# One comparison for sixteen steps' one-hots in the loop of a graph layer, with the second buffer in dead attention memory

## The reference, cut to what matters

```python
def _gcn_conv(x, W, b, src, dst, norm, num_nodes):
    h = x @ W
    msgs = h[src] * norm[:, None]
    out = jax.ops.segment_sum(msgs, dst, num_segments=num_nodes)
    return out + b
h = jax.nn.relu(_gcn_conv(x, W1, b1, src, dst, norm, n))
out = _gcn_conv(h, W2, b2, src, dst, norm, n)
```

## Time and profile before

| | before |
|---|---|
| median of 3 runs | 719.45 us (718.57 to 721.18) |
| profiled execution | 719.86 us |
| its span | 718.0 us |
| PE busy | 568.2 us, 79% |
| DVE busy | 502.6 us, 70% |
| ACT busy | 349.0 us, 49% |
| comparisons for one-hots (L672) | 128, 154.9 us |

### The profile page before, as it was taken

The page is one execution under the profiler, slowest core; times in us unless marked ns, Lnnn a source line. Parts: engine busy times, 40 slices in busy tenths (PEclk is TensorE's granted clock), DMA queues, the critical chain, the costliest instruction groups (busy, mean ns, idle before and its releaser), DMA issues.

```text
span 718.0 us, 13436 instructions
## 1 busy us (share of the span) xinstructions
PE 568.2 (79%) x4970; PEld 502.2 (70%) x4970; DVE 502.6 (70%) x1104; ACT 349.0 (49%) x625; POOL 132.9 (19%) x133
## 2 busy tenths in 40 slices
PE   0979983597999999999999999997540799999600
PEld 0235442586999999997899999997530699999500
DVE  6792988736999999995656646677541677878534
ACT  0023863457777777771211113232260598999400
POOL 2000000000000000000000000447566055656600
PEclk9998997689999999999999999999755699999955
DMA  7999999800424554100046775382423255555199
GB/s 177 247 284 283 283 283 282 295 0 1 169 118 174 230 230 172 59 2 1 1 196 263 303 324 205 125 284 75 129 69 84 79 150 144 150 162 145 37 241 294
DMA packets 80157, 121.16 MB, mean 169 GB/s; under 512 B 8573, under 2 KB 68770, under 8 KB 78429
## 3 DMA queue, kind: packets, MB, share of 16 engines
q1 hardware_dynamic: 70621, 107.03, 49.2%
q0 software_dynamic: 9472, 13.27, 5.7%
HBM read 50.00 MB, written 72.21 MB: 170 GB/s over the span
## 4 chain that ended last, share of the span: by engine, by line
PE 53%; DVE 21%; DMA 9%; issue 5%; ACT 5%; POOL 3%; SPq 1%; DVEq 1%; ACTq 0%; POOLq 0%
PE psB L1260 21%; DVE hot L672 7%; PE psC L1163 4%; PE psA L1175 3%; DMA back<-expert_out 3%; PE psC L1260 3%; POOL expert_slots L559 3%; DMA xs<-expert_slots 3%; PE psD L1175 3%; DMA acc<-in_x_dram 2%; PE psB L1447 2%; PE psD L1322 2%; PE psA L1435 1%; ACT counts L1492 1%; PE psC L1461 1%
## 5 line engine op out<-in xcount | busy, mean ns | idle before, releaser
L1260 PE MATMUL psB<-hs,counts 125*128 125x256 f16 x1600 | 210.7, 274 | 0.0
L1260 PEld LDWEIGHTS psB<-hs,counts 125*128 125x128 f16 x1600 | 172.3, 140 | 0.6
L672 DVE TENSOR_TENSOR hot<-iota_j,places 128x2048 bf16<-128x2048 bf16 x128 | 154.9, 1223 | 21.3 <-PE psA L1175 13.5
L551 POOL IOTA row_of<- 128x25 f32 x1 | 0.2, 237 | 421.8 <-DVE acc L722 421.8
L566 POOL DMA_INDIRECT expert_out<-y,to_row x64 | 66.4, 1037 | 62.0 <-DVE y L1101 49.7
L559 POOL DMA_INDIRECT expert_slots<-rows,place x50 | 62.2, 1244 | 64.4 <-issue 48.2
L1492 ACT CAST counts<-psA 128x1000 f16<-128x1000 f32 x64 | 63.3, 988 | 16.4 <-PE psA L1175 16.3
L1492 ACT CAST counts<-psD 128x1000 f16<-128x1000 f32 x64 | 63.5, 993 | 13.1 <-PE psD L1175 13.1
L1175 PE MATMUL psA<-hot 128*128 128x125 bf16 x512 | 50.3, 223 | 12.9 <-DVE hot L672 7.1
L1175 PEld LDWEIGHTS psA<-hot 128*128 128x128 bf16 x512 | 38.8, 99 | 22.9 <-DVE hot L672 12.4
L1163 PE MATMUL psC<-wcat,xnT 128*125 128x512 f32 x100 | 52.4, 650 | 1.8 <-ACT xnT L1479 1.8
(11 more groups left out here) (283 smaller groups left out, 1018.0 us busy)
## 6 DMA issues: line engine op xcount, KB each, us to landing
expert_slots<-zeros SPq DMA_DIRECT2D x8, 3536.0 KB, 30.2
kept_counts<-counts SPq DMA_DIRECT2D x6, 4000.0 KB, 12.5
counts<-kept_counts SPq DMA_DIRECT2D x6, 4000.0 KB, 12.3
xs<-expert_slots SPq DMA_DIRECT2D x32, 272.0 KB, 3.1
back<-expert_out SPq DMA_DIRECT2D x5, 1120.0 KB
w_raw<-in_L_ffn_w_dram SPq DMA_DIRECT2D x2, 2048.0 KB, 13.8
acc<-in_x_dram SPq DMA_DIRECT2D x1, 2800.0 KB
out_dram<-acc SPq DMA_DIRECT2D x5, 560.0 KB
```

Source lines behind the costliest of these rows:

```text
L672: v.tensor_tensor(hot[:, slot].rearrange("p g w n s -> p (g w) n s"), iota_j[:, :, :].unsqueeze(1).to_broadcast([P, 2 * pairs, P, PAIR]), ...
L1260: m = pe.matmul(sum_bank(g, d), counts5[0:PT, buf, a, d, :], hs2[0:PT, a, :, :].rearrange("p q f -> p (q f)"), start=first, stop=last, ski ...
```

## The change

In the loop, and only there, one comparison makes the one-hots of two units (sixteen steps), 4096 elements on a partition. It needs two buffers of twice the size. One is the whole of `hot`; the other lies in the q columns of sixteen rows of `qkv`, read as bf16, each row 256 elements long and 1540 bytes from the next. The comparison raises `hot_ready` by 2 at its end. DVE waits once ahead of the loop for the q transposes, and before each pair until the unit three before the pair's first is built.

```diff
+        wide_hot = (hot[:, :, :, :, :, :].rearrange("p u g w n s -> p (u g w) n s"),
+                    qkv[:, 0:4 * UNIT // PAIR, 0:HID].bitcast(BF16).rearrange("p m (n s) -> p m n s", s=PAIR))
+
+        def hot_of(unit):
+
+            block = UNIT // PAIR * 2
+            if unit < UNITS + 2:
+                at = unit % 2
+                return wide_hot[0][:, block * at:block * at + block]
+            return wide_hot[unit // 2 % 2][:, block * (unit % 2):block * (unit % 2) + block]
...
+            def hot_pair(unit):
+
+                pairs = 2 * UNIT // PAIR
+                column = P * FIRST_ORDER[unit // UNITS] + UNIT * (unit % UNITS)
+                val = places[:, column // PAIR:column // PAIR + pairs].rearrange("p g w s -> p (g w) s")
+                v.tensor_tensor(wide_hot[unit // 2 % 2], iota_j[:, :, :].unsqueeze(1).to_broadcast([P, 2 * pairs, P, PAIR]),
+                                val.unsqueeze(2).to_broadcast([P, 2 * pairs, P, PAIR]), ALU.is_equal).then_inc(hot_ready, 2)
...
+            v.wait_ge(q_transposed, len(TILE_GROUPS))
             for i in range(CH - 1):
                 k = FIRST_ORDER[i]
                 for r in range(UNITS):
                     unit = UNITS * (i + 1) + 2 + r
-                    if unit < UNITS * CH:
-                        v.wait_ge(built, 2 * unit - 2)
-                        hot_unit(unit % 2, unit)
+                    if unit < UNITS * CH and r % 2 == 0:
+                        v.wait_ge(built, 2 * unit - 4)
+                        hot_pair(unit)
...
-                bank = 512 * (j % 2)
+                bank, hots = 512 * (j % 2), hot_of(g // 2)
                 for q in range(GROUP):
                     pair, s = (GROUP * (j % 2) + q) // PAIR, q % PAIR
-                    m = pe.matmul(ps[:, bank + KEYS * q:bank + KEYS * q + KEYS], hot[:, slot, pair, 0, :, s], hot[:, slot, pair, 1, 0:KEYS, s],
+                    m = pe.matmul(ps[:, bank + KEYS * q:bank + KEYS * q + KEYS], hots[:, 2 * pair, :, s], hots[:, 2 * pair + 1, 0:KEYS, s],
```

More of the change, by code:

```diff
@@ L230, in gps_layer @@
             counts5 = counts[:, :, :, :].rearrange("p r s (a d) -> p r a d s", d=W)
+        wide_hot = (hot[:, :, :, :, :, :].rearrange("p u g w n s -> p (u g w) n s"),
[6 more added lines that the diff above has]
+            return wide_hot[unit // 2 % 2][:, block * (unit % 2):block * (unit % 2) + block]
+        assert (UNITS + 2) // 2 % 2 == 1
         until_experts.close()
@@ L1164, in project, with build @@
                 m.then_inc(projected, 1)
-            def build(g, j, slot, ps):
+            def build(g, j, ps):
                 if j % 2 == 0:
@@ L1189, in _ @@
                         g = 2 * (n - FIRST) + j
-                        build(g, j, (n - FIRST) % 2, (psA, psD)[(n - FIRST) % 2])
+                        build(g, j, (psA, psD)[(n - FIRST) % 2])
             def spread_scales():
@@ L1284, in _ @@
                     g = 2 * UNITS * (k + 1) + j
-                    build(g, j, j // 2 % 2, (psA, psD)[j // 2 % 2])
+                    build(g, j, (psA, psD)[j // 2 % 2])
                     while 2 * UNITS * due < (len(SUM_LIST) - 6) * (j + 1):
```

## The result

The changed kernel takes 726.12 us (median of 6 runs, 723.74 to 727.13) against 718.25 us (6 runs, 716.57 to 721.18) for the kernel before beside it: 1.0107 times as long, 95% interval 1.0078 to 1.0135. Slower, as forecast, and 0.5 us above the forecast time. The profiled execution took 726.33 us, its span 724.4.

What follows compares the result with a forecast made beforehand. PE was taken to bound the loop, with DVE close behind. Terms of 5.6 + 0.6 - 0.2 gave 6.0 us, 725.9 on the profiled execution, taken as 725.6 us; range 721.5 to 731.0.

Steps and rivals of the forecast that it cites:

- What bounds the loop: In the loop, PE sets the pace, busy 21.56 of 22.44 us a chunk; every microsecond it loses reaches the end.
- The pair's duration: On DVE, one double-width comparison takes 2.29 us, with bounds of 2.13 and 2.45.
- A: Unit 10 of each chunk: the wide pair behind the group 0 addition makes PE start 0.80 us later, +5.6 in all.
- B: Boundary between chunks: the second addition starts earlier, so PE starts the next unit 0 earlier, -0.16 us.
- C: Local unit 2 of the next chunk: its pair ends late behind the sums, +0.16 us, cancelling B at six boundaries.
- D: The loop's first comparison: the wide pair ends later than ACT's counts, so PE starts 0.6 us later.
- Throughput: Rival: DVE's total work sets the pace, pairs save 0.56 us a chunk, kernel faster at 715.5 us; chance 0.03.
- No change: Rival: the pair takes at most 1.52 us, so unit 10 isn't late; 718.5 us; chance 0.05.
- Dear rows: Rival: comparisons into qkv rows cost far more than forecast; 729.8 us, or some 732.2 by the skill's rate; chance 0.05.
- Lost double rate: Rival: qkv comparisons lose their double rate and take 4.42 us each; at least +42, 762 us; chance 0.02.
- Clock in the steady chunks: Rival: TensorE's clock falls in the new waits of 1.0 us, seven times; 735.5 us; chance 0.04.
- Released by DVE: Sign: PE idles about 1.0 us before local unit 10 and DVE ends that wait.

Runs made afterwards that it cites:

- e6_order: Changed kernel with the loop's first pair narrow and the sums moved behind the pairs PE needs next, on DVE and ACT: 711.43 us, 0.9914 of before.
- e3_split_first: Changed kernel with only the loop's first pair made by two narrow comparisons: 724.86 us, 1.0118 of the kernel before.
- e1_narrow: Changed kernel with its second buffer and longer lead kept, but every comparison as narrow as before: 715.89 us, 0.9992 of the kernel before.
- e4_before_late10: Kernel before plus one unread narrow comparison per chunk between the group 0 addition and unit 10's comparison: 723.36 us, 1.0093 of before.
- e2_split10: Changed kernel with only the pair of units 10 and 11 made by two narrow comparisons: 723.53 us, 1.0103 of the kernel before.
- e5_spare_work: Changed kernel plus one unread narrow comparison per chunk ahead of the group 0 sums on DVE: 724.30 us, 1.0100 of the kernel before.
- e8_split_rest: Changed kernel with units 10 to 15 of each chunk made by narrow comparisons, the others wide: 719.44 us, 1.0034 of the kernel before.
- e10_act_only: Changed kernel, first pair narrow, with ACT scaling the sums one or two casts later and DVE's order kept: 724.25 us, 1.0087 of before.

## Why the prediction was right

- **What bounds the loop.** PE's waits, of which each reaches the end: +7.47 us in the loop, with PE, DVE and ACT no busier. Right, and e6_order, which removes the waits and no work of PE, gives back 13.3 us of loop, 2.0 of them by its narrow first pair (e3_split_first).
- **The pair's duration.** 2.29 forecast, 2285 and 2287 ns measured. The 0.03 us for the strided rows were 0.002.
- **A, unit 10: +0.80.** From unit 2 to unit 10 the second chunk takes 11.53 us (192.58 to 204.11), before 10.74 (22.44 less 9.10 and 2.60): +0.79. The mechanism, one wide pair behind an addition that waits for ACT's copy, is shown by e1_narrow (no width, no loss), e4_before_late10 (lateness without width, the same loss) and e6_order (no lateness, width without loss). What I had not seen is that the pairs after unit 10 are late too, which didn't matter for the sum but made e2_split10 miss.
- **B, the boundary: -0.16.** From unit 10 to the next unit 0: 8.99 against 9.10, -0.11.
- **C, unit 2 of the next chunk: +0.16.** 2.69 us after unit 0 (189.89 to 192.58) instead of 2.60: +0.09, and +0.32 in the fourth chunk alone. B and C otherwise cancel, as said.
- **D, the first pair: +0.6.** The wait grew by 0.64 (3.62 against 2.98). But the first chunk grew by 2.66, where A, B and D as measured make 1.3 (0.79 - 0.11 + 0.64). This is the term that was too small, and the missing 1.3 to 1.4 us are the clock, which I had priced in the steady chunks alone. A narrow first pair leaves the first chunk 4.2 to 4.7 us longer than the steady one in nine profiles, a wide one 5.3 in e2_split10, e5_spare_work and e8_split_rest, and 6.3 in the changed kernel. The windows of the changed kernel behind its restart at 166.73:

```profile
166.70:168.00 1.30, 1.27 (x9) 1.06 (x10) 1.30 (x1) 0.14 (x1) 0.00 (x0) 0.50 0.00 0
...
170.00:172.00 2.00, 2.00 (x15) 1.67 (x14) 0.74 (x1) 0.81 (x1) 0.00 (x0) 0.50 0.00 0
172.00:172.50 0.50, 0.50 (x6) 0.40 (x4) 0.50 (x1) 0.18 (x1) 0.00 (x0) 0.58 0.00 0
172.50:173.50 1.00, 1.00 (x14) 0.98 (x13) 1.00 (x1) 0.41 (x1) 0.00 (x0) 1.00 0.00 0
```

  PE works at the 1.2 GHz level until 172.4, 5.7 us. From unit 2 to unit 10 this chunk takes 14.18 us (166.73 to 180.91) where the second takes 11.53, so 2.65 are lost. Before, it was 2.9 us at that level and 1.30 lost (169.06 to 181.10, 12.04, where a steady chunk takes 10.74). The 1.35 us between them and D's 0.64 come to 2.0; above the nine with a narrow pair, 4.46 in the mean, this first chunk stands out by 1.9. In e2_split10, behind the same wait of 3.62 us, the clock was low for only 3.4 us:

```profile
163.20:164.00 0.80, 0.75 (x9) 0.74 (x10) 0.80 (x1) 0.16 (x1) 0.00 (x0) 0.96 0.00 0
164.00:165.00 1.00, 1.00 (x9) 0.85 (x8) 1.00 (x1) 0.42 (x1) 0.00 (x0) 0.50 0.00 0
...
167.00:168.00 1.00, 1.00 (x11) 0.89 (x10) 0.80 (x1) 0.87 (x1) 0.00 (x0) 0.82 0.00 0
```

  So D is 0.8 us in three of four profiles (5.28 less 4.46) and 1.9 in one. In e5_spare_work and e8_split_rest, too, the low clock lasted 3.4 us. How often the longer stretch comes in runs without a profile stays open.
- **The sum.** 6.0 forecast; the loop gained 7.47, of which 1.4 are that stretch. The medians lie 7.9 apart, within the scatter of what lies outside the loop. That the forecast time was met to 0.5 us is in part luck: it started from 719.45, and the kernel before took 718.25 in the longer series, so 1.2 us of the loss that the forecast lacks don't show.
- **The rivals.** Throughput: e5_spare_work adds 1.13 us of DVE work a chunk at no cost. No change: the pair takes 2.29, not 1.52. Dear rows: 2 ns. The Trainium skill, Vector Engine (DVE) Microarchitecture Reference, section 5.2 Measured stream behaviour, gives its 1.30 ns for pairs of words that start on an odd word on both sources. The estimate of 2.79 us spread that over rows of 512 bytes at the output; the measurement, 2.29, decides, and these rows don't feel it. Lost double rate: a qkv pair takes 2.29 us, not 4.42. Clock in the steady chunks: granted 1.00 through waits of 0.98 us; wrong there, but alive at the loop's start. The Trainium skill, Perfetto Trace Analysis, section Optimizing Scalar/DVE Operations, says that breaking operations up may let work finish sooner where the engine isn't saturated but makes others wait; e1_narrow and e8_split_rest agree, 22.30 and 22.41 us against 23.20.
- **What I named as signs.** 55 comparisons, 0.98 us before unit 10, 0.46 at the boundary and 23.2 us a chunk all came. DVE's busy time did not stay much the same: it fell from 20.97 to 19.80 us a chunk. "Released by DVE" holds for the weight load and, by e10_act_only, in fact; the matmul's row says ACT.

## What to carry to other kernels

Before operations are merged, look for the first consumer behind an operation that waits for another engine: merging makes that consumer wait for the whole of the merged one, and a busy share of 93% (20.97 of 22.44 us) didn't mean that work saved there is time gained. An operation that waits for another engine belongs behind the work that the bottleneck needs next, on both engines of the chain at once: here this was worth 0.39 us a chunk with one buffer (22.44 to 22.05) and 0.70 with two (22.30 to 21.60), where the merging itself gave nothing. Of a wait with two candidates that end within 0.1 us, trust neither name; work out from the code which of them the instruction needs.

## What the runs showed of the hardware

A wide comparison into rows of 512 bytes that lie 1540 apart took 2287 ns, into rows that touch 2285. After similar idling of TensorE (2.98 and 3.62 us) the clock was granted at 0.50 (the 1.2 GHz level) for 3.4 us in twelve of the thirteen profiles and for 6.8 us in the changed kernel. In the kernel before (first line) and in the changed kernel (second line) it fell during the wait, before PE went on at 169.06 and 166.73:

```profile
168.32:168.82 0.50, 0.00 (x0) 0.00 (x0) 0.50 (x2) 0.50 (x2) 0.00 (x0) 0.69 0.00 0
```

```profile
165.35:165.85 0.50, 0.00 (x0) 0.00 (x0) 0.50 (x1) 0.50 (x2) 0.00 (x0) 0.74 0.00 0
```

In e2_split10 the first builds after the wait still ran at full speed (granted 0.96, four in 0.41 us), and the clock fell behind them.
